# A graph-transformer layer whose gather loop is preceded by a sort: the stage ahead of the loop rebuilt

## The reference

```python
xn = _layernorm(x, axis=-1)
q = (feats @ Wq.T + bq); k = (feats @ Wk.T + bk); v = (feats @ Wv.T + bv)   # feats = xn
qe = q[:, c, :]; ke = k[:, r, :]; ve = v[:, r, :]      # r = src, c = dst, per edge, 8 heads of 32
sim = jnp.einsum('hed,hed->eh', qe, ke) * scale        # scale = 32 ** -0.5
p = jnp.exp(sim - m[c]); attn = p / s[c]               # softmax over the edges of one dst
agg = segment_sum(attn * ve, c)
x = x + (agg @ Wo.T + bo) + mix(xn)
x = x + ffn(layernorm(x))                              # 8 experts, capacity 977
```

## Time and profile before

| | us |
|---|---|
| time, median of 3 runs (lowest to highest) | 3378.02 (3372.4 to 3378.71) |
| span of the profiled execution, first to last instruction | 2949.1 |
| median of the runs less that span | 428.9 |
| first gather of the loop, from the start of the span | 272.61 |
| last gather of the loop, starts at | 2382.2 |

### The profile page before, as it was taken

The page is one execution under the profiler, slowest core; times in us unless marked ns, Lnnn a source line. Parts: engine busy times, 40 slices in busy tenths (PEclk is TensorE's granted clock), DMA queues, the critical chain, the costliest instruction groups (busy, mean ns, idle before and its releaser), DMA issues. The chain is left out here.

```text
span 2949.1 us, 36213 instructions
## 1 busy us (share of the span) xinstructions
PE 2127.7 (72%) x9400; PEld 1712.6 (58%) x9401; DVE 2429.0 (82%) x3296; ACT 1010.5 (34%) x4314; POOL 2119.7 (72%) x2220
## 2 busy tenths in 40 slices
PE   5675777767776777767888876556666655599998
PEld 4473555555565666555666554444444435599997
DVE  5676788888888999999999888899999985366665
ACT  3220555556566666611111111011111114345353
POOL 4465777777777777777777777777777775567785
PEclk9796888998999999989999898887888885599999
DMA  6746777777777777788888887777777758423331
GB/s 218 246 156 172 208 210 208 207 211 217 219 218 219 218 219 218 227 233 241 257 255 257 254 241 213 212 211 211 211 211 211 211 162 288 152 70 76 88 92 15
DMA packets 257830, 587.19 MB, mean 199 GB/s; under 512 B 49410, under 2 KB 135505, under 8 KB 257565
## 3 DMA queue, kind: packets, MB, share of 16 engines
q0 software_dynamic: 150480, 467.10, 57.4%
q1 hardware_dynamic: 97947, 109.47, 11.2%
q10 hardware_dynamic: 9296, 9.44, 0.9%
HBM read 519.05 MB, written 71.76 MB: 200 GB/s over the span
## 5 line engine op out<-in xcount | busy, mean ns | idle before, releaser
L1041 POOL DMA_INDIRECT wide<-kv_d,arena x1099 | 1051.0, 956 | 335.0 <-issue 326.7
L1340 PE MATMUL ps<-wide,arena 128*128 128x264 f32 x2432 | 694.6, 448 | 238.9 <-DVE wide L1444 238.6
L1340 PEld LDWEIGHTS ps<-wide,arena 128*128 128x128 f32 x2432 | 530.2, 223 | 395.2 <-DVE wide L1444 283.4
L1041 POOL DMA_INDIRECT arena<-kv_d,arena x539 | 515.3, 956 | 164.3 <-issue 159.1
L1176 ACT ACTIVATE ps<-wide 128x256 f32 x229 | 88.8, 388 | 1324.2 <-DVE arena L1410 1282.5
L1413 DVE TENSOR_REDUCE arena<-arena 128x64 f32<-128x2048 f32 x229 | 523.5, 2286 | 7.9
L1340 PE MATMUL ps<-arena 128*128 128x264 f32 x1216 | 350.4, 451 | 128.7 <-DVE arena L1444 128.7
L1410 DVE TENSOR_TENSOR arena<-wide,ps 128x2048 f32<-128x2048 f32 x153 | 349.3, 2283 | 105.7 <-DMA wide<-kv_d,arena 105.6
L1340 PEld LDWEIGHTS ps<-arena 128*128 128x128 f32 x1216 | 267.0, 225 | 209.0 <-DVE arena L1444 152.9
L1444 DVE TENSOR_TENSOR wide<-wide,ps 128x2112 f32<-128x2112 f32 x152 | 356.8, 2347 | 24.4 <-ACT arena L1191 24.4
L141 PE MATMUL ps<-halves 128*128 128x256 f32 (+2 forms) x2304 | 361.9, 319 | 3.2 <-DVE halves L1703 1.6
(11 more groups left out here) (310 smaller groups left out, 3137.8 us busy)
## 6 DMA issues: line engine op xcount, KB each, us to landing
wide<-kv_d,arena POOLq DMA_INDIRECT x1099, 3.8
arena<-in_w SPq DMA_DIRECT2D x16, 1024.0 KB, 5.4
kv_d<-wide SPq DMA_DIRECT2D x49, 260.0 KB, 2.2
arena<-xn_d SPq DMA_DIRECT2D x82, 128.0 KB, 3.4
arena<-kv_d,arena POOLq DMA_INDIRECT x539, 3.8
hb_d<-arena SPq DMA_DIRECT2D x16, 516.0 KB
q_d<-wide SPq DMA_DIRECT2D x49, 128.0 KB, 2.7
xn_d<-arena SPq DMA_DIRECT2D x7, 896.0 KB, 9.0
```

The source lines that it names most:

```text
L1041: e.indirect_dma_start(out=kvb[k][:, j, :], out_offset=None, in_=kv_d, in_offset=bass.IndirectOffsetOnAxis(ap=ixb[k][:, j:j + 1], axis=0)) ...
L1340: m = e.matmul(psE[(k + 1) % 3][:, 0:264], ident, kvb[b][:, j, 256:ROW], start=(j == 0), stop=(j == J - 1))
```

## The change

1. *No padded copy.* `dst_d` goes. The block firsts are loaded from dst itself as SP's first transfers, and the histogram stands ahead of the normalising of group 0 on VectorE.
2. *Row gathers.* The 50 gathers are issued in one go as soon as the histogram is ready, with an offset in elements, on four semaphores.
3. *Counts by signs.* ScalarE takes the sign of (node - 1/2 - edge's dst), with the sum of a row as second output: two such instructions a tile from tile 7, three from tile 27, done at tile 30. The pointer is half the sum plus a constant (L402 of the changed kernel).
4. *The sort* starts at tile 31 with two steps a tile (`SORTED_FROM`), with 64 classes (`CLS`) in place of 128, in seven steps of eight columns; the product with the class matrix and its sum are two VectorE instructions a step. The own ids are gathered in one go.
5. *Query.* Its bias is added by TensorE as two matmuls of one row (`one_r` by `bq_hi` and `bq_lo`), and ScalarE copies it out of PSUM. The scale is folded into the weights' rounding; group 0 is centred by ScalarE too.
6. *Id stores* and the first 13 query gathers are issued behind the last tile (`first_queries`). The tables no longer wait for the stores.
7. *Blank rows* go once to `blank_d` in DRAM; sixteen copies from there to `hb_d` are issued by SP in the loop, two at the start of each of the eight rounds.

The core of the diff:

```diff
-        dma(Y, flat(dst_d)[0:E].rearrange("(a b) -> a b", b=825), dst.rearrange("(a b) -> a b", b=825), s_ed)
-        wait(Y, t_ed)
-        t_fi = dma(Y, fi_i, dst_d.rearrange("(a p) j -> p a j", p=128)[:, :, 0], s_fi, allow_slow_non_contiguous=True)
+        dma(Y, fi_i[:, 0:12], dst[0:whole].rearrange("(a p j) -> p a j", p=128, j=128)[:, :, 0], s_fi, allow_slow_non_contiguous=True)
...
+        wait(G, t_off)
+        for q, (c0, c1) in enumerate(QUARTERS):
+            for c in range(c0, c1):
+                s_row[q].inc(G.indirect_dma_start(out=rows[:, c, :], out_offset=None, in_=dst.rearrange("(a b) -> a b", b=825),
+                                                  in_offset=bass.IndirectOffsetOnAxis(ap=blki[:, c:c + 1], axis=1)), 16)
...
+                wait(S, (s_row[q], s_row[q].n), t_half)
+                counted[1] = a(S.activation(less[:, c, :], rows[:, c, :], ACT.Sign, bias=nodeh[:, c:c + 1], scale=-1.0,
+                                            accum_out=fine[:, c:c + 1]))
...
-                t = v(V.tensor_tensor(less[:, c0:c1, :], rows[:, c0:c1, :],
-                                      nodeid[:, c0:c1].unsqueeze(2).to_broadcast([128, c1 - c0, 128]), ALU.is_lt))
-                t = v(V.tensor_reduce(fine[:, c0:c1], less[:, c0:c1, :], AX.X, ALU.add))
...
-            for q in range(14):
+            for q in range(8):
-                        T.matmul(b[:, i * 128:(i + 1) * 128], start_[:, c:c + 1].to_broadcast([128, 128]), ident, start=True, stop=False)
-                        m = T.matmul(b[:, i * 128:(i + 1) * 128], trib, OHc[:, c, :], start=False, stop=True)
+                        T.matmul(b[:, i * CLS:(i + 1) * CLS], start_[0:CLS, c:c + 1].to_broadcast([CLS, 128]), ident[0:CLS, 0:CLS],
+                                 start=True, stop=False)
+                        m = T.matmul(b[:, i * CLS:(i + 1) * CLS], trib, OHc[:, c, :], start=False, stop=True)
-                        t = read[u] = v(V.scalar_tensor_tensor(out=of_rank[:, i, :], in0=ps[5 + 2 * (u % 2)][:, i * 128:(i + 1) * 128], scalar=1.0,
-                                                               in1=OHc[:, c, :], op0=ALU.mult, op1=ALU.mult, accum_out=rankf[:, c:c + 1]))
+                    t = read[u] = v(V.tensor_tensor(of_rank[:, 0:n, :], r3(ps[5 + 2 * (u % 2)][:, 0:n * CLS], CLS), OHc[:, 8 * u:8 * u + n, :], ALU.mult))
+                    t = v(V.tensor_reduce(rankf[:, 8 * u:8 * u + n], of_rank[:, 0:n, :], AX.X, ALU.add))
...
+        def first_queries():
+            wait(Y, *t_own_)
+            dma(Y, ids_of[:, 0:32, 256:QI], own[0].bitcast(f32), s_own)
+            t_ids = dma(Y, ids_of[:, 32:NT, 256:QI], own[1].bitcast(f32), s_own)
+            wait(G, *t_sorted, t_ids, *t_kv)
...
+                    m = product(b1_[:, 0:256], [(one_r, bq_hi), (one_r, bq_lo)], first=False)
+                    t_qe[u] = a(S.activation(stage[u % 3][:, 520:776], b1_[:, 0:256], ACT.Copy))
-                    t_bias[u] = v(V.tensor_tensor(stage[u % 3][:, 520:776], b1_[:, 0:256], bal[:, 512:768], ALU.add))
-                        t_hz = dma(Y, hb_d[i * 512:(i + 1) * 512, :].rearrange("(p j) d -> p (j d)", p=128), empty, s_hz)
...
+            def blanks():
+                e.dma_start(hb_d[bass.ds(val(e, hz, H * CP - 512), 512), :].rearrange("(p j) d -> p (j d)", p=128), blank_d).then_inc(s_hz.h, 16)
```

More of the change, by code:

```diff
@@ L287, in gps_layer_kernel @@
         t_src = dma(Y, src_d[NB:NBP, :], zero[0:NBP - NB, 0:128].bitcast(i32), s_pz)
+        assert E + 86 == NB * 128
+        wait(Y, t_em)
+        t_bl = dma(Y, blank_d, blank, s_bl)
         st = take(42)
@@ L306, in root @@
             return inverse_root(rs[:, 0:n], r3(mv, 2)[:, 0:n, 1])
-        def center(xt, i, o=None):
-            wait(V, (sv, sv.n))
-            o = xt if o is None else o
-            return v(V.tensor_scalar(out=o[:, i, :], in0=xt[:, i, :], scalar1=mv[:, 2 * i:2 * i + 1],
-                                     scalar2=rs[:, i:i + 1], op0=ALU.subtract, op1=ALU.mult))
-        def norm(xt, n, o=None):
-            spread(xt, range(n))
-            wait(V, root(n))
-            for i in range(n):
-                last = center(xt, i, o)
-            return last
-        wait(V, t_x[0])
-        t_n = {(0, 6): norm(xbuf[0], 7)}
-        NB13 = 13
         quot, hi, lo, over = [R1[:, 16 * i:16 * i + NB13] for i in range(4)]
@@ L389, in pump, with ranks @@
                     more[0] = None
-        def take_rows(t_blk):
-            wait(G, t_blk, t_ed)
-            for c in range(50):
-                s_row.inc(G.indirect_dma_start(out=rows[:, c, :], out_offset=None, in_=dst_d,
-                                               in_offset=bass.IndirectOffsetOnAxis(ap=blki[:, c:c + 1], axis=0)), 16)
-                if c % PER_TILE == PER_TILE - 1:
-                    yield
-        def take_own(t_rp):
-            wait(G, t_rp, t_src)
+        def ranks():
+            wait(V, counted[1])
+            t = v(V.scalar_tensor_tensor(out=rp, in0=fine, scalar=0.5, in1=half, op0=ALU.mult, op1=ALU.add))
+            wait(V, t)
+            v(V.tensor_tensor(deg[:, 0:NT], rp[:, 1:50], rp[:, 0:NT], ALU.subtract))
+            t = v(V.tensor_copy(rpc[:, 0:NT], rp[:, 0:NT]))
+            wait(G, t, t_src)
             for c in range(NT):
@@ L574, in tables @@
             t_ds = v(V.tensor_copy(permS[:, 0:NT], fx))
-            while not t_kv:
-                yield
-            assert t_own_
-            wait(V, t_hz, *t_own_, *t_kv)
-            t_q49 = v(V.memset(qi[:, NT, :], 0.0))
-            wait(G, t_q49, t_ds, *t_own_, *t_kv)
-            for c in range(FIRST_Q):
-                (s_q0 if c < RING else s_q).inc(G.indirect_dma_start(out=qi[:, c, :], out_offset=None, in_=q_d,
-                                                                     in_offset=bass.IndirectOffsetOnAxis(ap=permS[:, c:c + 1], axis=0)), 16)
+            t_sorted.append(t_ds)
+            t_sorted.append(v(V.memset(qi[:, NT, :], 0.0)))
+            wait(V, t_bl, t_src)
             yield
@@ L751, in gps_layer_kernel @@
                 pt = ps[6]
-                wait(T, t_n[grp, j] if grp else t_n[0, 6], t_xT.get(t - 1), t_id)
+                wait(T, t_n[grp, j], t_xT.get(t - 1), t_id)
                 for k in range(2):
@@ L761, in gps_layer_kernel @@
                 t_lo[t] = v(V.tensor_tensor(lo_, xnT[:, t, :, :], hi_.bitcast(f32), ALU.subtract))
-                if t > WAIT_ROWS:
-                    pump()
+                landed = max([c for u_, c in LANDED if t >= u_], default=0)
+                count_some(min(2 + (t >= LANDED[3][0]), landed - counted[0]))
+                if t == SORTED_FROM:
+                    assert counted[0] == 50
+                    more[0] = ranks()
+                pump()
                 if t > 0:
```

198 lines of the change are left out of this document (106 added, 92 removed).

## The result

The changed kernel takes 3480.55 us, median of four runs (3473.3 to 3483.64), against 3377.0 for the kernel before on the same chip (four runs): a ratio of 1.0309, 95% interval 1.0294 to 1.0323. It is **slower by 3.1%, 104 us**, where 3361 and a gain were forecast. The profiled execution took 3479.68 us with a span of 3478.5.

A forecast was written before the change was run, and what follows sets the result against it. Taken as bound by back-to-back loop gathers, so the 272.6 us stage ahead counts in full: -24.3 us to the last tile, +7.5 tail, copies 0, sum -16.8; span 2932, time 3361 us, range 3338 to 3386.

The forecast's parts named there:

- the price of the unpaced gathers: Stage ahead of the loop: 50 row gathers need 63 us, end near 77, and VectorE's 6.76 us wait for rows goes.
- the last rival: Change does not do what it says: counting was hidden anyway, own gathers become the limit, ending near 200 us; chance 0.03.
- T: Time at which the last tile leaves, ahead of the loop: 245.26 us before, 221 forecast, -24.3 us.
- the base of the sum: Sum made against the profiled span, 2949.1 us; the runs' median, 428.9 us above it, taken as unchanged.
- Ranks: From last class offset read to ranks standing, 40.1 us before: seven steps and four tiles, 32 us (22 to 34).
- Tail: Last tile's end to first loop gather: 35 us instead of 27.35 with ids stored late, +7.5 us (+5 to +11).
- Tiles: Two one-row matmuls added per tile cost 0 to 0.26 us, taken as 0.24; TensorE's tile becomes 2.54 us.
- product 0: Tile 0's product at the kernel's start: begins near 22.5 us instead of 25.82, -3.3 us (-6 to +2).
- ScalarE is not the pace: Against the rival that signs of 0.5 us and unhidden handovers make tiles 2.9 us or more; chance 0.10, half of it slower.
- the copies cost 0: Blank-row copies in the loop costed at 0, 0 to 57 us in all; rival of held-up gathers, chance 0.09.
- the end follows the first loop gather: Loop gathers run back to back, so an earlier or later first one shifts the kernel's end by as much.
- the tail eats it: Rival: ids land at T + 14 and T falls by only 12 us; balance about -1, no change; chance 0.10.

The follow-up runs named there:

- the second trace of before: Kernel before with no edit, traced again in an execution that was also timed: 3345.5 us, ratio 0.9972; traced execution 3346.03 us, span 3344.9.

## Why the prediction was wrong

1. **The step that failed is the price of the unpaced gathers, which the sum puts at nothing for every engine but GpSimd.** "the gathers, unpaced from about 14 us, need 50 x 1.26 = 63 us and end near 77" is right for GpSimd (14.7 to 77.3), but the sum has no term for what it does to the other engines: 37 us, and 59 us for the own gathers, of which the last rival said only that they end ahead of T. Paced, the two trains give back 88 of the 104 us lost. No rival had them as a burden on TensorE.
2. **Behind it stands the base of the sum**: "the median of the runs shown is 428.9 us above it, which I take as unchanged". Those 428.9 us were no fixed part outside the span. In the second trace of before they are 396.9 (3346.03 less 2949.1): 363.6 in the loop, 12.1 ahead of it, 20.1 behind, and 1.1 outside the span. The loop's part did stay (2473.2 and 2494.5 us, on two chips), though its gathers are 1.51 us apart on average and not 1.26. In the stage it depends on how densely gathers are issued beside the work of other engines, which is what the change alters. The difference stood in the table of the profile; the rows that were priced come from an execution that did not have the effect.
3. *Ranks*: 32 us forecast, 58.0 measured (243.12 to 301.16), 55.9 with paced gathers. The range per class, from half of 0.49 to 0.49 us, did not allow a class to become dearer; with the granted clock below 0.7 it does. 22 us of the loss.
4. *Tail*: +7.5 us forecast. With both paced, the end of the last tile (270.4) to the first loop gather (311.9) is 41.5 us against 27.4 in the second trace of before: +14. The first query gather comes at T + 13.8, not T + 10.5, and the masks meet the second and third query gather (5.92 and 2.62 us), not the fifth and sixth; with 128 classes they meet the sixth and seventh, and the tail is 38.9 us. The mechanism was right, the size was too small by half.
5. *Tiles*: 0.24 us forecast for the two matmuls, 0.6 measured (2.90 against 2.30). The term was mis-sized, at no cost to the end, as its removal shows.
6. *What held*: product 0 starts at 22.64 (22.5 forecast); VectorE no longer waits for rows; the signs are done at tile 30; ScalarE is not the pace (about 0.38 us from sign to sign); the copies cost 0; the end follows the first loop gather (with both paced 81.5 us earlier, 88 us by the ratios). None of it decided the sign.

With trains paced and 128 classes the whole rebuilding stands at 0.9982 [0.9963, 1.0], within what two equal kernels differ by. By its trace the last tile ends at 244.0 instead of 257.4, 13.4 us earlier, and the longer tail takes 11.6 of them: the rival "the tail eats it", whose balance was -1, is what is left of the change without its trains and its classes. The pacing that the kernel before had was worth more than all that the change brought.

Two slips in the prediction change nothing: its 49 "classes" in the ranks' price are 49 columns, and half of ScalarE's 0.10 is 0.05, where the chance of slower counts 0.06.

**Open.** Whether the loop's idle time has the same cause as the stage's: it has the same mark, but nothing was tried there. By what way gathers delay the updates of TensorE's semaphore; no experiment here reaches further. Why the execution of before that the prediction read had none of this. Its trace holds 475 updates of TensorE's semaphore of the stage for 474 instructions that give one, the second trace of before only 426, so the recording may itself have a part in it; that was not tested. Whether TensorE's lower clock with 64 classes comes from the form of the matmuls or from how they lie beside the tiles; the two were not separated.

## What to carry to other kernels

Compare the profile's span with the timed runs before pricing anything from it: a gap of 13% is time that the trace does not hold, and a change may move it. Where a long idle time ends with "issue" or "remote", look in the program for what is waited for, and in the rows for when that had ended. A row of indirect gathers has a price for the engines beside it that stands in no row of its own; keep it in small groups with a pause behind them, and try the group's size: two instead of three, with the counts a little later, gave 0.6% here. Halving a matmul's size need not shorten it: read the granted clock of the stretch along with the busy share.

## What the hardware showed unexpectedly

- Twenty gathers issued 1.26 us apart in 25 us cost the tiles beside them 21 us, with 512 or with 4 bytes a row (50.64 and 50.46 us for ten tiles, 29.36 without); twenty memsets on the same engine did not (30.04).
- Beside unpaced gathers the updates of TensorE's semaphore came 27 and 43 us behind the end of its products (62.12 for 35.08, 85.30 for 42.48), and the waiting engines started within 0.03 us of them.
- One execution of the kernel before ran its loop in 2109.6 us (span 2949.1), the one of the second trace in 2473.2, and all 21 timed ones beside it have spans of 3340 to 3363 us.
- A TensorE that is busy for 10 of 10 us ran at a granted clock of 0.56 to 0.69 for 50 us with 64-column matmuls among its work, and at 1.00 with 128-column ones.
